# Four tail lanes, a shorter rounding to the 6-bit grid, and a re-costed planner in a two-layer transformer kernel

## Chip, core and metric

The kernel runs on one core of a Trainium2 chip. The metric is the device time of one execution in microseconds (us), the median of several executions. The engines are called as in the profile: PE (TensorE matmuls, with PEld its weight loads), DVE (VectorE), ACT (ScalarE), POOL (GpSimd) and SP (SyncE, which issues most DMAs).

## What is computed

Input `x` has 8 batches of 512 tokens with 128 features. All of it is float32. Two layers are applied; each batch is independent except for the routing, whose results do not depend on how batches are grouped.

```python
# layer 0: for each of two uses of the same experts, with attention between them
z = layernorm(x)
x = x + 0.5 * moe(z)          # 8 experts, best 2 of 8 by router logits, softmax over the two
x = x + attention(layernorm(x))  # 16 heads of width 8, rotary positions, causal softmax
x = x + 0.5 * moe(layernorm(x))
# moe: h = relu(z @ W1[e] + b1[e]); y = h @ W2[e] + b2[e]; weighted by the gate
# layer 1, the "tail": mx linear, gated scan block with its own ffn, mx linear
x = x + 0.5 * mxlinear(layernorm(x))
x = x + gated(layernorm(x))
x = x + 0.5 * mxlinear(layernorm(x))
# mxlinear: blocks of 32 features, scale = max|block| / 7.5,
#   q = nearest value on the 64-value grid (3 mantissa bits, 2 exponent bits; ties to the lower value)
#   out = (q * scale) @ (weight, quantized the same way).T + bias
# gated: xn = rmsnorm(z); a = 0.998 * sigmoid(xn Wd + bd) + 0.001
#   h_t = a_t h_(t-1) + sigmoid(xn Wg + bg) * tanh(xn Wv + bv)      (scan over the 512 tokens)
#   z2 = z + h;  out = z2 + Wout(silu(rms(z2) Wgate) * (rms(z2) Wup))
```

## The kernel before

**Stages.** The work is cut into stages, each a chain of steps on given engines (table `STAGES`: a letter for the engine and a cost in us, with `+` for what lands later and `<` for other predecessors). The mixture of experts (MoE) runs in six phases (`ORDER`): use 1 of batches 0-1, 2-4, 5-7 and use 2 of batches 0-2, 3-5, 6-7. A phase routes its tokens (`prep`, `route`), writes them with indirect DMAs on POOL into slots sorted by expert in HBM (`scat`, L1481), works through blocks of 256 slots, of which there are 106 in all (`wload` loads the expert's weights, 1 MB, into one of four buffers `wt`; `zin` loads and transposes the tokens; `hid` is one half of the hidden layer, two to a block; `res` the second matmul; `yout` transposes back and stores), and gathers the results with indirect DMAs on POOL (`comb`, L1493). Attention has the stages `proj`, `stack`, `maxi`, `mrow`, `scor`, `val` and `heads`; the last instruction of a batch's attention is the addition at L1131. Weights are split once at the start into two halves of float32r and stored in HBM scratch (`sload`, `split`).

**Order.** `timetable()` simulates all steps with their costs, a greedy list scheduler with the longest remaining chain as priority. Its result is one list of steps; every engine's program is the part of the list with its letter, written out in that order (`follow`). The engines are in order, so an instruction that waits holds up all behind it on its engine. `follows()` gives the dependences between stages and `bank_of` assigns the six shared PSUM banks.

**Tail.** The tail of a batch is `mxa`, then `gated`, then `mxb` (L1183-1263 on DVE, L1395-1450 on ACT, L1519-1556 on POOL, L815-868 on PE). It works in six buffers `tb[b % 2]` of 128x512 and small statistics in `sm_f[b % 2]`. There are two such sets ("lanes"): batch b waits for `mxb` of batch b-2. In an mx unit (there are 16, two a batch) ACT normalizes, DVE finds the block maxima (`scaled`, L1134-1141), POOL multiplies by the reciprocals (L1531), ACT takes the absolute value (L1405), DVE rounds with nine operations on 128x512 (`nearest`, L1143-1162), POOL multiplies by the scales (L1535), and adds half the bias to x (L1538), PE transposes and multiplies with the quantized weight, DVE adds to x (L1205). In `gated`, after the scan, DVE takes the mean square of z2 with bn_stats (L902, called at L1238-1239), and three small operations (L1242-1246); the unit ends in the addition to x at L1262.

**Start.** SP issues, in this order, the small inputs, ten DMAs that fill the slot scratch with zeros (L468), the first four expert loads (L487-488), the loads of the later inputs (`later`), and then alternates stores of split weights (L495) with the other four expert loads. All stages that need zeros wait for one semaphore that counts all ten.

```python
for f in range(2):
    for i in range(0, SLOTS, 1024):
        n = min(1024, SLOTS - i)
        e.dma_start(zd[f][i:i + n]..., zeros[...]).then_inc(l_zero, 16)
```

## Time and profile before

| what | value |
|---|---|
| median of 3 executions | 1385.29 us (1380.07 to 1401.86) |
| the profiled execution | 1396.99 us |
| its span in the profile | 1395.3 us |
| PE busy | 1012.7 us, 73% |
| DVE busy | 873.2 us, 63% |
| ACT busy | 628.3 us, 45% |
| POOL busy | 537.5 us, 39% |
| granted PE clock, mean | 0.849 of full speed |
| HBM traffic | 217.33 MB, mean 156 GB/s |

The span is measured on the profiler's clock from first to last event; the execution's own time is 1.7 us longer. Busy times of engines overlap, so they don't add up to the span. A "releaser" is what ended an engine's wait.

### The profile page before, as it was taken

The numbers are of one execution on the slowest core, as the hardware profiler recorded it, in microseconds if no ns is written. First come the engines' busy times: TensorE is split into PE (matmuls) and PEld (weight loads), VectorE is DVE, ScalarE is ACT, GpSimd is POOL, SyncE is SP. The second block draws the span as 40 slices with busy tenths as digits, with TensorE's granted clock in tenths as the row PEclk, the third lists the DMA queues.
The fourth block names the chain that finished last, engine by engine and source line by source line (L and its number), as shares of the span: only waits on it lengthen the run. The fifth ranks groups of instructions, "written<-read, shape, count | busy, mean of one in ns | idle before, by whom it ended". The sixth has DMA issues, their size and how long they took to land.

```text
span 1395.3 us, 21086 instructions
## 1 busy us (share of the span) xinstructions
PE 1012.7 (73%) x6869; PEld 717.2 (51%) x6869; DVE 873.2 (63%) x2457; ACT 628.3 (45%) x1341; POOL 537.5 (39%) x730
## 2 busy tenths in 40 slices
PE   1058885879899997799899648989991386664273
PEld 1048875655655764346567635646571356643132
DVE  5536474647665767457564446866659777858646
ACT  2135653345464664345467324636751363452241
POOL 2424245227221125565122472332428722344312
PEclk9999997899898998589899869968995698886576
DMA  9958987664554533534355756714114243410000
GB/s 334 353 211 289 320 297 238 210 222 145 164 173 137 171 108 87 175 113 133 107 167 192 262 153 192 239 61 135 54 54 158 68 152 117 163 29 14 15 0 16
DMA packets 84461, 217.33 MB, mean 156 GB/s; under 512 B 14848, under 2 KB 43392, under 8 KB 69760
## 3 DMA queue, kind: packets, MB, share of 16 engines
q1 hardware_dynamic: 76160, 199.18, 42.6%
q0 software_dynamic: 8192, 16.79, 4.1%
q8 instruction: 56, 0.92, 0.3%
q14 instruction: 53, 0.43, 0.1%
HBM read 160.86 MB, written 54.53 MB: 154 GB/s over the span
## 4 chain that ended last, share of the span: by engine, by line
PE 52%; DVE 11%; DMA 11%; issue 9%; POOL 8%; ACT 5%; SPq 4%; POOLq 0%; DVEq 0%; ACTq 0%
PE bank L584 46%; PE bank L596 5%; POOL z_scratch L1481 4%; DMA Qs<-q_scratch 4%; DMA q_scratch<-ab 2%; DMA tb<-in_wr 1%; DMA zin<-z_scratch 1%; SPq L542 1%; POOL yg L1493 1%; DVE sm_m L1090 1%; SPq L554 1%; DMA z_scratch<-zb,pos 1%; ACT tb L1277 1%; DMA k_scratch<-ab 1%; PE bank L731 1%
## 5 line engine op out<-in xcount | busy, mean ns | idle before, releaser
L1090 DVE TENSOR_REDUCE sm_m<-bank 128x4 f32<-128x512 f32 x320 | 212.1, 684 | 114.2 <-PE bank L584 113.9
L1515 POOL TENSOR_SCALAR_AFFINE_SELECT P<-P 128x256 f32<-128x256 f32 (+1 forms) x320 | 118.7, 377 | 348.4 <-ACT P L1367 344.8
L1367 ACT ACTIVATE P<-bank 128x512 f32<-128x512 f32 x320 | 179.8, 598 | 104.2 <-PE bank L584 103.4
L584 PE MATMUL bank<-zh,wt 128*128 128x256 f32 x1272 | 203.5, 310 | 14.9 <-DVE zh L1021 5.8
L1029 DVE SCALAR_TENSOR_TENSOR hlo<-bank,hhi 128x512 fp32r<-128x512 f32 x212 | 144.4, 687 | 101.9 <-ACT hhi L1316 101.2
L584 PEld LDWEIGHTS bank<-zh,wt 128*128 128x128 f32 x1272 | 178.8, 210 | 27.5 <-issue 12.3
L1316 ACT ACTIVATE hhi<-bank 128x512 fp32r<-128x512 f32 x212 | 125.9, 598 | 102.8 <-PE bank L584 97.2
L584 PE MATMUL bank<-hhi,wt 128*128 128x256 f32 x848 | 160.1, 313 | 5.4 <-ACT yb L1324 5.4
L1481 POOL DMA_INDIRECT z_scratch<-zb,pos x128 | 128.8, 1006 | 84.3 <-DVE pos L1010 49.2
L1493 POOL DMA_INDIRECT yg<-y_scratch,pos x128 | 124.6, 974 | 90.6 <-issue 54.1
L584 PE MATMUL bank<-Ks,Qs 32*128 32x256 f32 (+2 forms) x512 | 110.3, 447 | 66.7 <-DMA Qs<-q_scratch 53.6
L584 PEld LDWEIGHTS bank<-hhi,wt 128*128 128x128 f32 x848 | 121.9, 200 | 20.1 <-issue 18.1
L596 PE MATMUL bank<-ident,tb 128*128 128x128 f32 x160 | 34.0, 352 | 135.0 <-POOL tb L1535 99.8
L584 PEld LDWEIGHTS bank<-Ks,Qs 32*128 32x128 f32 x512 | 50.1, 200 | 120.9 <-issue 46.6
L584 PE MATMUL bank<-Qs,Ks 34*128 34x256 f32 (+2 forms) x512 | 87.2, 411 | 24.6 <-DVE sm_m L1090 10.5
L584 PE MATMUL bank<-P,Va 128*16 128x512 f32 (+3 forms) x1024 | 99.7, 488 | 0.0
L596 PEld LDWEIGHTS bank<-ident,tb 128*128 128x128 f32 x160 | 23.7, 180 | 145.4 <-issue 61.1
L1324 ACT ACTIVATE yb<-bank,wt 128x256 f32<-128x256 f32 x106 | 50.3, 474 | 106.7 <-PE bank L584 106.2
L584 PE MATMUL bank<-hlo,wt 128*128 128x256 f32 x424 | 89.0, 292 | 11.6 <-DVE hlo L1029 11.6
L584 PEld LDWEIGHTS bank<-Qs,Ks 34*128 34x128 f32 x512 | 45.3, 203 | 64.1 <-issue 31.5
L584 PEld LDWEIGHTS bank<-hlo,wt 128*128 128x128 f32 x424 | 68.8, 199 | 13.0 <-DVE hlo L1029 13.0
L584 PE MATMUL bank<-mask,identb 128*128 128x128 bf16 x512 | 72.5, 238 | 0.0
(184 smaller groups left out, 1694.6 us busy)
## 6 DMA issues: line engine op xcount, KB each, us to landing
wt<-w_scratch SPq DMA_DIRECT2D x106, 1025.0 KB, 6.5
zin<-z_scratch SPq DMA_DIRECT2D x106, 128.0 KB
y_scratch<-yt SPq DMA_DIRECT2D x106, 128.0 KB
w_scratch<-wt SPq DMA_DIRECT2D x8, 1024.0 KB, 9.3
q_scratch<-ab SPq DMA_DIRECT2D x32, 256.0 KB
k_scratch<-ab SPq DMA_DIRECT2D x32, 256.0 KB
Ks<-k_scratch SPq DMA_DIRECT2D x64, 128.0 KB, 2.8
Qs<-q_scratch SPq DMA_DIRECT2D x64, 128.0 KB, 3.1
```

The source lines that it names most:

```text
L542: e.dma_start(dst[par, :, 8 * r:8 * r + 8, :], (ab[3], ab[0])[low][:, :]).then_inc(s_qk[par], 16)
L554: e.dma_start(dst[64 * s_:64 * s_ + 32, :, :].bitcast(F32), src[b % 2, HH * g + s_:HH * g + HH:2].rearrange("p r t -> r p t")).then_inc(l_ ...
L584: return e.matmul(o, lhs, rhs, start=start, stop=stop, **kw)
L596: t = e.transpose(o[:, j * 128:(j + 1) * 128], src[:, j, :], ident[:, :])
L1029: e.scalar_tensor_tensor(out=hlo[s % 4][:, :, :].rearrange("p c t -> p (c t)"), in0=shared("hid", s, 0), scalar=0.0, in1=hhi[s % 4][:, :, ...
L1090: e.tensor_reduce(bn_m[:, k, s_, :], blocks(shared("maxi", i, 0, s_)), AX.X, ALU.max).then_inc(*d_max.step(i, f"m{s_}"))
L1316: e.activation(hhi[s % 4][:, :, :].rearrange("p c t -> p (c t)"), shared("hid", s, 0), ACT.Relu).then_inc(*a_hid.step(s, "hi"))
L1324: e.activation(yb[u % 2][:, :], y_bank[:, 0:SB], ACT.Identity, bias=wt[u % WR][:, 2048:2049].bitcast(F32)).then_inc(*a_yout.step(u, "y"))
L1367: e.activation(P[:, (2 * i + s_) % PR, :], shared("scor", i, 0, s_), ACT.Exp, scale=SCALE).then_inc(*a_sc.step(i, f"e{s_}"))
L1481: e.indirect_dma_start(zd[f % 2], bass.IndirectOffsetOnAxis(ap=pos[:, f % 2, k, i:i + 1], axis=0), zb[:, q % ZR, i % 4, :], None).then_inc ...
L1493: e.indirect_dma_start(yg[t % YR][:, k, :], None, yd[f % 2][0:SB * PHASE[f].blocks], bass.IndirectOffsetOnAxis(ap=pos[:, f % 2, k, i:i + 1 ...
L1515: e.affine_select(out=v, in_=v, compare_op=ALU.is_ge, fill=0.0, base=0, channel_multiplier=-1, pattern=pattern).then_inc(*p_sc.step(i, f"m ...
```

## The change

The diff does seven things.

1. The tail gets four lanes instead of two. Lanes 0 and 1 have five buffers `tb` each, lanes 2 and 3 lie in `P`, the buffer of attention's exponentials, and their first step waits for the last `val`. `TAIL_LANE` names each batch's lane; a batch waits for the one before it in its lane.
2. `nearest` is written anew with seven operations: the bits of the exponent are masked out and bounded by 1.0 (two one-input operations), and five operations with two inputs do the rounding. It needs no absolute value, so the ACT step L1405 goes. It works in three buffers.
3. The bias of the mx linear is added by PE: one more 128x512 matmul of `top` (a matrix with ones in its first row) with the bias, into the bank of the product. The POOL step L1538 goes.
4. The mean square of z2 comes from four ACT activations (Square, with the sum as second output), in place of bn_stats, bn_aggr and two small operations on DVE.
5. The zero fill is split: four DMAs of phase 0's slots, after the first four expert loads; the other six after all eight, behind `later`. Each part has its own semaphore.
6. All costs in `STAGES` are new. SP's steps cost by bytes (a weight load was 0.3 and is 2.6, a store of q or k was 0.4 and is 3.2), most PE steps cost more (`hid` 0.72, now 0.94), many DVE steps less.
7. Small things: raw rows of the eight expert loads go through four places of which one is in `tb0`; the memsets of `Ks` move behind the first routing; six slot limits instead of four are compared in `route` (L998).

```diff
+def pieces_of(f, start, end):
+    return [(f, i, min(1024, end - i)) for i in range(start, end, 1024)]
+FIRST_FILL = pieces_of(0, 0, PHASE[0].blocks * SB)
+LATER_FILL = pieces_of(0, PHASE[0].blocks * SB, SLOTS) + pieces_of(1, 0, SLOTS)
+TAIL_LANE = (0, 1, 0, 2, 3, 1, 0, 2)
+TAILS = max(TAIL_LANE) + 1
+def lane_before(b):
+    return max([p for p in range(b) if TAIL_LANE[p] == TAIL_LANE[b]], default=-1)
...
-    "wload": ("S.3+6", [], 1),
-    "hid": ("P.72 A.6 D.7", [(0, 2)], 1),
+    "wload": ("S2.6+4", [], 1),
+    "hid": ("P0.94 A0.58 D0.66", [(0, 2)], 1),
...
+                lane = TAIL_LANE[u] if stage in ("mxa", "gated", "mxb") else u % lanes
...
-        tb = [[sb(f"tb{i}{j}", [128, 4, 128]) for j in range(6)] for i in range(2)]
+        tb = [[sb(f"tb{i}{j}", [128, 4, 128]) for j in range(5)] for i in range(2)]
+        lane_t = [[t[:, :, :] for t in lane] for lane in tb]
+        lane_t += [[P[:, 5 * i + j, :].rearrange("p (j c) -> p j c", c=128) for j in range(5)] for i in range(2)]
...
+                if n == SG - 1:
+                    fill(FIRST_FILL, l_zero0)
+                if n == NE - 1:
                     later()
+                    fill(LATER_FILL, l_zero)
...
+                    mm(blocks(o), top[:, :], biasb.unsqueeze(1).to_broadcast([128, 4, 128]), True, False, skip_group_check=True)
                     w.wait_ge(*a_wq.at(0, "w"))
                     w.wait_ge(*a_mx[v].at(b, "zt"))
...
-                e.tensor_scalar(p, r, 2.0, 0.125, ALU.is_ge, ALU.mult).then_inc(*f.step(u_, "p"))
-                e.tensor_scalar(q, r, 4.0, 0.25, ALU.is_ge, ALU.mult).then_inc(*f.step(u_, "q"))
-                e.scalar_tensor_tensor(out=st, in0=p, scalar=0.125, in1=q, op0=ALU.add, op1=ALU.add).then_inc(*f.step(u_, "st"))
-                e.scalar_tensor_tensor(out=p, in0=st, scalar=MAGIC, in1=u, op0=ALU.mult, op1=ALU.add).then_inc(*f.step(u_, "r1"))
-                e.scalar_tensor_tensor(out=r, in0=st, scalar=-MAGIC, in1=p, op0=ALU.mult, op1=ALU.add).then_inc(*f.step(u_, "r2"))
-                e.tensor_tensor(p, r, u, ALU.subtract).then_inc(*f.step(u_, "d1"))
-                e.scalar_tensor_tensor(out=q, in0=p, scalar=2.0, in1=st, op0=ALU.mult, op1=ALU.is_ge).then_inc(*f.step(u_, "d2"))
-                e.tensor_tensor(q, q, st, ALU.mult).then_inc(*f.step(u_, "d3"))
-                e.tensor_tensor(r, r, q, ALU.subtract).then_inc(*f.step(u_, "d4"))
+                e.tensor_scalar(r.bitcast(U32), u.bitcast(U32), 0x7F800000, None, ALU.bitwise_and).then_inc(*f.step(u_, "p"))
+                e.tensor_scalar(r, r, 1.0, None, ALU.max).then_inc(*f.step(u_, "e"))
+                e.scalar_tensor_tensor(out=t, in0=r, scalar=MAGIC / 8, in1=u, op0=ALU.mult, op1=ALU.add).then_inc(*f.step(u_, "r1"))
+                e.scalar_tensor_tensor(out=u, in0=r, scalar=(MAGIC + 1) / 8, in1=u, op0=ALU.mult, op1=ALU.add
+                                       ).then_inc(*f.step(u_, "r2"))
+                e.scalar_tensor_tensor(out=u, in0=r, scalar=-0.125, in1=u, op0=ALU.mult, op1=ALU.add).then_inc(*f.step(u_, "r3"))
+                e.scalar_tensor_tensor(out=t, in0=t, scalar=1.0, in1=u, op0=ALU.mult, op1=ALU.min).then_inc(*f.step(u_, "mn"))
+                e.scalar_tensor_tensor(out=t, in0=r, scalar=-MAGIC / 8, in1=t, op0=ALU.mult, op1=ALU.add).then_inc(*f.step(u_, "r"))
...
-                stats(T[0], sm_, f, b, ("bn3", "ag3"))
-                e.tensor_tensor(t_, mv[:, :, 0], mv[:, :, 0], ALU.mult).then_inc(*f.step(b, "t4"))
-                e.tensor_tensor(t_, t_, mv[:, :, 1], ALU.add).then_inc(*f.step(b, "t5"))
+                w.wait_ge(*a_ga.at(b, "sq"))
+                e.tensor_scalar(t_, t_, 1.0 / D, 1e-6, ALU.mult, ALU.add).then_inc(*f.step(b, "t6"))
...
+                for j in range(4):
+                    t = e.activation(T[4][:, j, :], T[0][:, j, :], ACT.Square, accum_out=sm_[:, 44 + j:45 + j])
...
-                e.activation(flat(T[5]), flat(T[1]), ACT.Abs).then_inc(*f.step(b, "abs"))
-                e.tensor_tensor(x, x, hbias.unsqueeze(1).to_broadcast([128, 4, 128]), ALU.add).then_inc(*f.step(b, "x"))
```

**What moves.** The first place is SP's start. `z_scratch` is the slot memory, `w_scratch` the split weights, `P<-in_w` and `tb<-in_wr` the raw weights of an expert. Before:

```order
L463 DMA tb<-in_wt 128x128
L468 DMA z_scratch<-P 128x1024 x4
L468 DMA z_scratch<-P 128x768
L468 DMA z_scratch<-P 128x1024 x4
L468 DMA z_scratch<-P 128x768
L470 DMA w_scratch<-small 128x8x2
L487 DMA P<-in_w 128x1024
```

And in the changed kernel, from the same place (of the four expert loads the last is shown):

```order
L505 DMA tb<-in_wt 128x128
L507 DMA w_scratch<-small 128x8x2
L529 DMA P<-in_w 128x1024
...
L530 DMA tb<-in_wr 128x512
L512 DMA z_scratch<-P 128x1024 x3
L512 DMA z_scratch<-P 128x768
L540 DMA w_scratch<-wt 128x2048 x3
```

The first expert load stands in front of the zeros instead of behind all ten of them, and only four fills stand before the first weight store.

The second place is PE where attention ends: `wo,ob` is its last product, of batch 7; `zin` and `yb` are transposes of a block, `zh`, `hhi` and `hlo` its products, `tb` a tail buffer. Before:

```order
L584 MATMUL bank0<-tb02,wga 128x512
L584 MATMUL bank6<-tb12,wga 128x512
L584 MATMUL bank2<-hhi2,wt1 128x256 x4
L584 MATMUL bank2<-hlo2,wt1 128x256 x2
L584 MATMUL bank1<-wo,ob 128x128 x4
L584 MATMUL bank3<-zh0,wt2 128x256 x6
L584 MATMUL bank2<-hhi3,wt1 128x256 x4
L584 MATMUL bank2<-hlo3,wt1 128x256 x2
```

In the changed kernel:

```order
L629 MATMUL bank2<-hhi3,wt1 128x256 x4
L629 MATMUL bank2<-hlo3,wt1 128x256 x2
L641 MATMUL bank6<-ident,yb0 128x128 x2
L629 MATMUL bank0<-wo,ob 128x128 x4
L641 MATMUL bank4<-ident,zin0 128x128 x2
L641 MATMUL bank7<-ident,zb 128x128 x4
L641 MATMUL bank1<-ident,yb1 128x128 x2
L641 MATMUL bank3<-ident,zin1 128x128 x2
```

Before, two batches were already in the middle of `gated` here (`tb02,wga`), and 30 of the 212 `hid` halves stood behind this place; now no `gated` has begun, and 46 halves stand behind it, of phases 4 and 5.

The third place is PE near the end. `tb0x` is lane 0, `tb1x` lane 1, `P` lanes 2 and 3; `wdT` is the mx weight, `wg3` and `wga` weights of `gated`. Before, the last `mxa` units and the start of the last two `gated`:

```order
L584 MATMUL bank3<-wdT,tb01 128x128 x4
L596 MATMUL bank4<-ident,tb10 128x128 x4
L584 MATMUL bank0<-wdT,tb11 128x128 x4
L596 MATMUL bank6<-ident,tb01 128x128 x4
L596 MATMUL bank1<-ident,tb11 128x128 x4
L584 MATMUL bank7<-tb02,wg3 128x512
L584 MATMUL bank3<-tb12,wg3 128x512
```

Now:

```order
L629 MATMUL bank7<-P,wga 128x512
L641 MATMUL bank0<-ident,tb01 128x128 x4
L629 MATMUL bank4<-P,wup 128x512
L641 MATMUL bank1<-ident,tb11 128x128 x4
L629 MATMUL bank0<-tb02,wg3 128x512
L641 MATMUL bank1<-ident,P 128x128 x4
L629 MATMUL bank0<-tb12,wg3 128x512
L629 MATMUL bank1<-P,wg3 128x512
```

Three batches (6, 5 and 7) begin `gated` together, while a fourth (batch 4, `P,wga`) is in its second half; before it was two at a time. Behind the last `zin` stand the tails of batches 4 to 7 whole, and the ends of 1, 2 and 3.

## Rows read from the trace of the kernel before

**Rows 1.** Busy time by stretch: start:end, length, PE, PEld, DVE, ACT, POOL, PEclk, DMA, GB/s.
```profile
870.00:1040.00 170.00, 158.17 (x1097) 101.92 (x1096) 112.88 (x296) 103.17 (x219) 53.61 (x96) 0.89 0.34 111
1040.00:1130.00 90.00, 36.96 (x231) 30.56 (x230) 74.28 (x220) 30.47 (x69) 62.61 (x60) 0.68 0.36 119
1130.00:1240.00 110.00, 80.56 (x491) 66.55 (x490) 82.57 (x203) 54.64 (x123) 29.17 (x26) 0.87 0.34 118
1240.00:1396.00 156.00, 70.53 (x260) 44.41 (x260) 100.54 (x257) 42.65 (x92) 55.62 (x51) 0.63 0.05 14
```

**Rows 2.** Waits after 1040 us: who for whom, total us, times, longest.
```profile
PE bank L596 <- POOL tb L1535: 99.8, 8, 24.1
```

**Rows 3.** Timeline of DVE: start, us, instruction; ends of attention and of lane pairs.
```profile
1030.14 0.69 DVE L1131 TENSOR_TENSOR xs<-xs,bank 128x512 f32<-128x512 f32 x1 [0.22 <-PE bank L584]
...
1293.42 0.69 DVE L1205 SCALAR_TENSOR_TENSOR xs<-bank,xs 128x512 f32<-128x512 f32 x1 [1.85 <-PE bank L584]
...
1391.14 0.69 DVE L1205 SCALAR_TENSOR_TENSOR xs<-bank,xs 128x512 f32<-128x512 f32 x1 [3.38 <-PE bank L584]
```

**Rows 4.** Timeline of the start: SP's queue and the first block on PE.
```profile
16.34 1.47 SPq L487 DMA_DIRECT2D P<-in_w  x1
...
73.50 4.47 SPq L529 DMA_DIRECT2D wt<-w_scratch  x4
...
87.70 0.69 PE L596 MATMUL bank<-ident,zin 128*128 128x128 f32 x2 [3.50 <-DMA zin<-z_scratch]
```

**Rows 5.** PE busy by tile: wt, then yb (whole span), tb (870:1040), tb (870:1396).
```profile
0.00:1396.00 1396.00, 404.90 (x2544) 0.85 0.47 156
...
0.00:1396.00 1396.00, 43.35 (x212) 0.85 0.47 156
...
870.00:1040.00 170.00, 27.24 (x93) 0.89 0.34 111
...
870.00:1396.00 526.00, 157.82 (x624) 0.77 0.26 85
```

**Rows 6.** PE groups, whole span: busy, mean ns; two records to a matmul.
```profile
L584 PE MATMUL bank<-tb,wg 128*128 128x512 f32 x48 | 24.2, 635 | 0.8 <-ACT tb L1426 0.8
```

**Rows 7.** DVE groups, 870:1396: busy us, mean ns, idle before.
```profile
L1160 DVE TENSOR_TENSOR tb<-tb 128x512 f32<-128x512 f32 x16 | 18.0, 1127 | 0.5
...
L1158 DVE SCALAR_TENSOR_TENSOR tb<-tb 128x512 f32<-128x512 f32 x16 | 14.7, 919 | 0.6
...
L1151 DVE SCALAR_TENSOR_TENSOR tb<-tb 128x512 f32<-128x512 f32 x16 | 12.2, 762 | 0.5
...
L1153 DVE SCALAR_TENSOR_TENSOR tb<-tb 128x512 f32<-128x512 f32 x16 | 11.1, 692 | 0.5
...
L902 DVE BATCH_NORM_STATS2 sm_f<-tb 128x6 f32<-128x128 f32 x32 | 7.0, 281 | 0.3
...
L1147 DVE TENSOR_SCALAR tb<-tb 128x512 f32<-128x512 f32 x16 | 6.7, 418 | 0.0
```

**Rows 8.** DVE busy by tile: hlo (whole span), then tb (870:1040).
```profile
0.00:1396.00 1396.00, 144.36 (x212) 0.85 0.47 156
...
870.00:1040.00 170.00, 29.14 (x48) 0.89 0.34 111
```

**Rows 9.** POOL groups, whole span: busy us, mean ns, idle before and releasers.
```profile
L1493 POOL DMA_INDIRECT yg<-y_scratch,pos x128 | 124.6, 974 | 90.6 <-issue 54.1 <-DMA y_scratch<-yt 31.0 <-DVE xs L1044 3.6
```

**Rows 10.** Timeline of POOL and DVE in the last mx units.
```profile
1283.95 1.43 POOL L1535 TENSOR_TENSOR tb<-tb,sm_f 128x512 f32<-128x512 f32 x1 [8.51 <-DVE tb L1162]
...
1285.96 1.64 DVE L1160 TENSOR_TENSOR tb<-tb 128x512 f32<-128x512 f32 x1
```

**Rows 11.** Waits before 1040 us: who for whom, total us, times, longest.
```profile
PE bank L584 <- DMA Qs<-q_scratch: 53.6, 11, 25.4
```

**Rows 12.** ACT on yb by stretch; the count is of MoE blocks finished.
```profile
1040.00:1130.00 90.00, 0.94 (x2) 0.68 0.36 119
1130.00:1240.00 110.00, 6.12 (x13) 0.87 0.34 118
```

More of the change, by code:

```diff
@@ L187, in timetable @@
             share, _, late = item[1:].partition("+")
-            steps.append((item[0], float(share), float(late or 0.15), [int(x) for x in after.split(",")] if after else [k - 1]))
+            steps.append((item[0], float(share), float(late or 0.12), [int(x) for x in after.split(",")] if after else [k - 1]))
         plan[stage] = (steps, {x[0]: len(x) - 1 for x in holds}, {b: (x[0], i) for x in holds for i, b in enumerate(x[1:])})
@@ L191, in timetable @@
             for k, step in enumerate(steps):
-                queues.setdefault((stage, u % lanes, step[0]), []).append((u, k))
+                lane = TAIL_LANE[u] if stage in ("mxa", "gated", "mxb") else u % lanes
+                queues.setdefault((stage, lane, step[0]), []).append((u, k))
     before, after = {}, {}
@@ L290, in sem, with flow, tail_flow @@
             return ctx.enter_context(nc.semaphore(name))
-        def flow(name, steps, lanes=1):
-            return Flow([sem(f"{name}_{i}") for i in range(lanes)], steps)
+        def flow(name, steps, lanes=1, lane_of=None):
+            return Flow([sem(f"{name}_{i}") for i in range(lanes)], steps, lane_of)
+        def tail_flow(name, steps):
+            return flow(name, steps, TAILS, TAIL_LANE)
         bank = [ctx.enter_context(nc.psum_tensor(f"bank{i}", [128, 512], F32)) for i in range(8)]
@@ L463, in begin, with fill @@
                 e.dma_start(flat(tb[0][1])[:, 0:128], a["wt"]).then_inc(l_const, 16)
-                w.wait_ge(*p_init.at(0, "zero"))
-                for f in range(2):
-                    for i in range(0, SLOTS, 1024):
-                        n = min(1024, SLOTS - i)
-                        e.dma_start(zd[f][i:i + n].rearrange("(p j) d -> p j d", p=128), zeros[:, 0:n // 128, :]).then_inc(l_zero, 16)
                 w.wait_ge(l_first, 64)
                 e.dma_start(wd[:, 2048:WROW].rearrange("(e p) c -> p e c", p=128), bt).then_inc(s_bias, 16)
+            def fill(parts, done):
+                w.wait_ge(*p_init.at(0, "zero"))
+                for f, i, n in parts:
+                    e.dma_start(zd[f][i:i + n].rearrange("(p j) d -> p j d", p=128), zeros[:, 0:n // 128, :]).then_inc(done, 16)
             def later():
@@ L1015, in route @@
                 e.tensor_scalar(ei[:, f % 2, :], fl, part, None, ALU.add).then_inc(*g.step(f, "ei"))
+                if f == 0:
+                    for i in range(QR):
+                        e.memset(Ks[i][32:34, :, :].bitcast(F32), 1.0)
+                        t = e.memset(Ks[i][96:98, :, :].bitcast(F32), 1.0)
+                    t.then_inc(*d_init.step(0, "keys"))
                 yield
@@ L1625 @@
     small[:, 44] = g["L1_attn_rms_ffn_w"]
[L1626 removed]
+    small[:, 45:45 + EB] = SB * np.arange(EB)[None, :]
     small[:, 0:KB] = np.arange(KB)[None, :]
```

227 lines of the change are left out of this document (116 added, 111 removed), and 41 rows, old and new, of the table STAGES.

## The prediction

> **What bounds the kernel now.** I read the table of stretches first, then the waits after 1040 us, then DVE's timeline for the ends of units. The reader is to see two kernels in one. Up to the end of attention, whose last addition is at 1030.1 us [rows 3], PE sets the pace: in the last stretch before, it is busy 158.2 of 170 us, a share of 0.93 [rows 1]. From 1040 on no engine is full. PE is busy 37.0, 80.6 and 70.5 of 90, 110 and 156 us, DVE 74.3, 82.6 and 100.5, and the granted clock falls to 0.68 and 0.63 where PE is least busy [rows 1]. PE waits there 99.8 us for the multiplication by the scales on POOL, which comes behind the rounding on DVE [rows 2]. That is a chain of dependent steps, and only two batches at a time are allowed to be in it. The last pair shows its length: from the end of the pair before (the L1205 at 1293.4) to its own end (1391.1) it is 97.7 us [rows 3], and the pairs follow one another. So 356 us go by with some 190 us of PE's work and 257 of DVE's.
>
> **The change part by part.**
>
> *Start.* The first expert load is issued at 16.3 us behind the zeros; the split weights are read back from 73.5 on, and the first block is transposed at 87.7 [rows 4]. The bytes to move before the first weights can be read are nearly the same as before, since all eight stores must be done. So at most the way from 73.5 plus a load's landing to 87.7 is open. I bound the gain by 0 and 14 us and take 5, by the third of it in which routing and scatter no longer come last. The moved `Ks` memsets and the wider compare in the routing count for nothing: they lie under the loads.
>
> *Attention's end.* The new order leaves 46 `hid` halves behind attention instead of 30, that is 8 blocks more, and moves the parts of batches 0 and 1 behind it. A block costs PE (404.9 + 2 x 43.4) / 106 = 4.64 us, where `zin` is taken to cost what `yb` does [rows 5]; 8 of them are 37.1. The tail's matmuls before 1040 are 27.2 [rows 5]. With PE at 0.93 this comes off about one to one: 1030.1 - 37.1 - 27.2 - 5 = 960.8. What the new costs do to the order inside the first 960 us I set at zero, with -54 us as one end (all of PE's waits for `Qs` gone [rows 11]) and +30 as the other, half of those waits added.
>
> *Work behind it.* PE has 23 blocks x 4.64 = 106.7, the tail's 157.8 [rows 5], and the sixteen new bias products. Such a product is a 128x512 matmul; of that form 24 cost 24.2 us busy [rows 6], so 16 cost 16.1. It stands before the wait for the transposed input and can be done early, but it is PE's time all the same. The sum is 280.6.
> DVE has today's 257.4 [rows 1], the 29.1 of batches 0 and 1 [rows 8], 8 blocks at 144.4 / 106 = 1.36 for the residue of the hidden layer [rows 8], and loses: the old rounding costs 2 x 0.42 + 4 x 0.70 + 0.76 + 0.92 + 1.13 = 6.45 a unit, where 0.70 stands for L1149, L1153, L1156 and L1162, of which L1153 is shown [rows 7]. The new one costs 2 x 0.42 + 5 x 0.69 = 4.30, if masking bits costs what L1147 does. The trace has no such integer operation: its bounds are 0.42 and 0.69 (an operation with two inputs), and I take 0.42 because it also has one input in SBUF; the other end adds 16 x 0.27 = 4.3 us of DVE. The gain is 16 x 2.15 = 34.4, and 7.0 for the statistics of z2 [rows 7]. DVE's sum is 257.4 + 29.1 + 10.9 - 41.4 = 256.0, so PE is now the fuller engine, though by little. ACT loses its absolute values and gets 32 small Squares; POOL loses 16 additions of x. Neither is near its limit (54.6 of 110 us for ACT at its fullest in the tail [rows 1]), so I put nothing for them. The Squares stand in the chain in place of the statistics: both have four operations on 128x128, and I call it even.
>
> *Four lanes.* A waiting step of a lane is now covered by three others. The new wait of lanes 2 and 3 for the last `val` costs nothing, since no batch of theirs is ready before attention ends. How full can PE be? The bounds are the two rows: 0.93 in the attention stretch and 80.6 / 110 = 0.73, the best that two lanes with blocks beside them reach [rows 1]. I take 0.85, nearer to the row in which PE has as many independent chains. 280.6 / 0.85 = 330.1.
>
> *Sum.* 960.8 + 330.1 = 1290.9; from the last addition to the end of the span it is 1395.3 - 1391.8 = 3.5 us now, and the execution's own time is 1.7 longer than the span: 1296.1. The profiled execution (1396.99) lies 0.8% above the median (1385.29), so against the median the forecast is 1285. With 0.93 it is 1257, with 0.73 it is 1339. Between those ends lies the forecast's own range, 1257 to 1339.
>
> *A cross-check by the chain.* Before the last block PE has the 106.7 and about two batches' tail, 2 x 174 / 8 = 43.5, which at 0.93 end at 960.8 + 161.5 = 1122. Sixteen gathers at 0.97 + 0.30 us [rows 9] bring 1143. Then batches 5, 6 and 7 run together: the pair's 97.7 less 4 x 2.15 for the rounding is 89, and a third batch adds half of its DVE work, some 13. That ends at 1245 and makes 1240 by the median: the chain no longer sets the end, but it is not far away, and one cannot come below it by filling PE better.
>
> **The ports of DVE and POOL.** In the last mx units a subtraction-like operation of DVE took 1.64 us beside POOL's L1535 at 1.43 [rows 10], against 0.69 for the undisturbed form [rows 7]; the means of L1158 and L1160, 0.92 and 1.13, hold such cases. The new rounding has five such operations in a row with two inputs, and four lanes put more of POOL's products beside them. The price by rows: 32 products, each of which stretches one operation by 1.64 - 0.69 = 0.95, are 30 us of DVE, and (256 + 30) / 0.85 = 336, 6 us over the forecast's 330; if half of it also falls on the chain, 21 us.
> The Trainium skill, page "SBUF — State Buffer", section "Who interferes with whom", says that a DVE instruction with two SBUF inputs contends with a GpSimd instruction that reads SBUF, and that the later one is blocked until the other is done. The trace agrees for this pair. By that rule every product of POOL hits the rounding of some other lane, and the time would be the 1306 of the rival below.
>
> **The rivals.**
> *A, the front gains too.* For it: PE waited 53.6 us in eleven places for `Qs` [rows 11], and the new costs give the DMAs of q and k real lengths. Against it: the data are needed when they are, and PE is at 0.93 in the last stretch already. It gives 1285 - 53 = 1232.
> *B, the ports.* As above: 1285 + 21 = 1306. For it are rows 10; against it is that a third of POOL's tail work (the additions of x) goes.
> *C, the lanes do not overlap.* PE and DVE are both near 0.85 by my sum, the engines are in order, and one late step of one lane holds up the three others. For it: two lanes reached only 0.73 with blocks beside them [rows 1]. Then the gain is that of the shorter units and of 0.73: 1339. This is also the time if the change doesn't do what it says.
> *D, slower.* 23 blocks now run behind attention, in the same queues as the tails. If each is held up by a tail's waiting step in front of it on PE, the last `comb` is late, and three batches' tails come behind it. In 1040 to 1130 just 2 blocks were finished in 90 us, in 1130 to 1240 it was 13 in 110, 8.5 us each [rows 12]. At 8.5 the last block is done at 960.8 + 195 = 1156, harmless. With T for the last block's end, the time is T + 21 + 102 + 5.2, so 1413 by the median (1425 by the profiled one) is reached at T = 1297, 14.6 us a block. At 15 it is 1422. Against it: a wait of a lane used to be long because there was no other, and this is what the change fills.
>
> **How the numbers follow.** Chances: the forecast 0.58, A 0.14, B 0.08, C 0.14, D 0.06. The predicted time is 1285. The range 1228 to 1348 takes in the forecast's 1257 to 1339, A and B, and C with its upper neighbours; it leaves out D, and the far side of A, with the start's full 14 us. A difference of 2% is about what a measurement of this kernel can tell from no change, so the borders are 1357.6 and 1413. Faster: 0.58 + 0.14 + 0.08 and most of C, 0.91. The same: what is left of C and the mild side of D, 0.04. Slower: 0.05.
>
> **What would show it.** The last addition of attention should come near 961 us (935 to 990). If it stays near 1030, the step on the 8 blocks is wrong; if it is near 910, A is right. Behind it PE should be busy about 280 us at a share of 0.85, with a granted clock over 0.8; a share under 0.75 means C. The wait of PE for POOL's product by the scales should fall from 99.8 to under 40 us. The rounding's two-input operations should have means near 0.69; 0.9 and more means B. `zin` should be reached first near 83 us. DVE's sum over the span should fall from 873 to about 830. The last `comb` should be over before 1170; after 1290, D is right. The prediction is wrong if the time is above 1348 although attention ended before 990, since then the fill of the tail was misjudged.

## The result and the profile after

Before, the median is 1389.09 us over 4 executions (1380.07 to 1401.86); the changed kernel's is 1266.72 over 4 (1255.51 to 1273.9). The ratio is 0.913, with a 95% interval of 0.903 to 0.924: faster by 8.7%. The forecast was 1285, a ratio of 0.928.

The profiled execution took 1273.9 us, its span is 1272.2. These are lines of its page, the last one PE's busy tenths in 40 slices:

```profile
span 1272.2 us, 21017 instructions
PE 1025.4 (81%) x6901; PEld 716.8 (56%) x6901; DVE 829.4 (65%) x2344; ACT 622.9 (49%) x1388; POOL 507.7 (40%) x714
PE   1048789688999999879999996988999789853884
```

The longest waits of PE up to the end of attention, and the one for `Qs` (who for whom, total us, times, longest):

```profile
PE bank L641 <- ACT zb L1319: 51.3, 5, 35.6
PE bank L641 <- DMA zin<-z_scratch: 31.2, 8, 13.8
...
PE bank L629 <- DMA Qs<-q_scratch: 4.8, 1, 4.8
```

PE has 13 us more work than before (1025.4 against 1012.7) in 123 us less time. The wait for `Qs` that was 53.6 us [rows 11] is 4.8. The next rows are the table of stretches, with the columns of [rows 1]: up to attention's last addition, from there to the last gather, the rest, and the last two together.

```profile
0.00:955.00 955.00, 791.49 (x5569) 541.14 (x5569) 580.26 (x1680) 457.71 (x967) 373.09 (x585) 0.88 0.57 192
955.00:1119.00 164.00, 142.79 (x902) 115.06 (x903) 124.92 (x353) 103.14 (x261) 84.16 (x85) 0.96 0.58 197
1119.00:1272.00 153.00, 91.08 (x431) 60.59 (x429) 124.22 (x313) 62.01 (x163) 50.46 (x46) 0.81 0.04 13
955.00:1272.00 317.00, 233.88 (x1332) 175.64 (x1332) 249.15 (x665) 165.15 (x423) 134.62 (x130) 0.89 0.32 108
```

The same cut of the kernel before:

```profile
0.00:1031.00 1031.00, 815.63 (x5846) 569.64 (x5847) 609.09 (x1761) 495.21 (x1047) 389.04 (x593) 0.89 0.56 186
1031.00:1396.00 365.00, 197.06 (x1025) 147.54 (x1023) 264.08 (x697) 133.13 (x295) 148.41 (x137) 0.72 0.21 71
```

Of the 123 us by which the span is shorter, 76 were won before attention's end and 47 behind it. In front, PE's busy time fell by only 24 us (815.6 to 791.5), but its idle time fell by 52 (215.4 to 163.5). Behind, PE does 37 us more work in 47 us less, and the granted clock is 0.89 instead of 0.72. As in [rows 1], the clock fell where PE is least busy: 0.96 with PE at 0.87, 0.81 with PE at 0.60.

The part with blocks beside the tails (955 to 1119) is nearly full now. The last 153 us are not. This is their table of stretches:

```profile
1119.00:1130.00 11.00, 9.63 (x79) 8.78 (x77) 10.18 (x41) 5.37 (x14) 3.95 (x4) 1.00 0.02 6
1130.00:1182.00 52.00, 19.60 (x84) 13.13 (x84) 49.67 (x116) 14.64 (x40) 19.69 (x18) 0.70 0.04 16
1182.00:1243.00 61.00, 51.18 (x218) 30.76 (x218) 42.32 (x116) 35.66 (x97) 18.68 (x18) 0.92 0.00 1
1243.00:1272.00 29.00, 10.67 (x51) 7.92 (x50) 22.05 (x44) 6.35 (x15) 8.15 (x7) 0.69 0.10 36
```

Batches go through the tail in threes, in step. From 1130 to 1182 six mx units come in two groups of three (the last of three batches, the first of three others): DVE is busy 49.7 of 52 us and PE 19.6. Then the last three batches and one more are in `gated`, and PE is busy 51.2 of 61 us. In the last three mx units it is DVE again, 22.1 of 29, and PE 10.7. The step shows on DVE's timeline:

```profile
1250.99 1.15 DVE L1198 TENSOR_SCALAR tb<-tb 128x512 f32<-128x512 f32 x1
1252.17 0.69 DVE L1200 SCALAR_TENSOR_TENSOR tb<-tb 128x512 f32<-128x512 f32 x1
1252.78 0.42 DVE L1196 TENSOR_SCALAR P<-P 128x512 uint32<-128x512 uint32 x1
1253.23 0.43 DVE L1198 TENSOR_SCALAR P<-P 128x512 f32<-128x512 f32 x1
...
1257.09 0.68 DVE L1202 SCALAR_TENSOR_TENSOR tb<-tb 128x512 f32<-128x512 f32 x1
1257.80 1.42 DVE L1205 SCALAR_TENSOR_TENSOR tb<-tb 128x512 f32<-128x512 f32 x1
...
1268.27 0.69 DVE L1250 SCALAR_TENSOR_TENSOR xs<-bank,xs 128x512 f32<-128x512 f32 x1 [1.59 <-PE bank L629]
```

The roundings of three batches stand directly behind one another, and DVE hardly waits; the last line is the kernel's last addition. PE's timeline shows the other side, one wait for each group of three:

```profile
1144.84 1.09 PE L641 MATMUL bank<-ident,tb 128*128 128x128 f32 x4 [11.85 <-POOL tb L1577]
...
1173.64 1.09 PE L641 MATMUL bank<-ident,tb 128*128 128x128 f32 x4 [17.65 <-POOL tb L1577]
...
1258.73 1.11 PE L641 MATMUL bank<-ident,tb 128*128 128x128 f32 x4 [14.57 <-POOL tb L1577]
```

### The profile page after: what moved, and what is told of

It is laid out like the page before. It is cut to its first block, busy times and chain, and to the rows that moved or that the text cites. A ratio compares the mean times of both kernels' runs of the same rounds, so it can differ in the third digit from the quotient of the medians.

```text
span 1272.2 us, 21017 instructions
## 1 busy us (share of the span) xinstructions
PE 1025.4 (81%) x6901; PEld 716.8 (56%) x6901; DVE 829.4 (65%) x2344; ACT 622.9 (49%) x1388; POOL 507.7 (40%) x714
## 4 chain that ended last, share of the span: by engine, by line
PE 42%; DVE 20%; DMA 13%; issue 8%; ACT 7%; POOL 6%; SPq 5%; DVEq 0%; ACTq 0%; POOLq 0%
PE bank L629 37%; PE bank L641 4%; DMA yg<-y_scratch,pos 3%; DMA zin<-z_scratch 2%; POOL z_scratch L1525 2%; DMA q_scratch<-ab 2%; DVE hlo L1079 2%; DVE sm_m L1140 2%; POOL yg L1537 2%; DMA w_scratch<-wt 2%; SPq L587 1%; PE bank L776 1%; SPq L610 1%; ACT P L1410 1%; ACT zb L1319 1%
## 5 line engine op out<-in xcount | busy, mean ns | idle before, releaser
L1140 DVE TENSOR_REDUCE sm_m<-bank 128x4 f32<-128x512 f32 x320 | 209.3, 684 | 101.6 <-PE bank L629 100.9
L1410 ACT ACTIVATE P<-bank 128x512 f32<-128x512 f32 x320 | 174.8, 594 | 110.6 <-PE bank L629 110.2
L629 PE MATMUL bank<-zh,wt 128*128 128x256 f32 x1272 | 209.1, 314 | 19.4 <-DVE zh L1071 13.3
L1559 POOL TENSOR_SCALAR_AFFINE_SELECT P<-P 128x256 f32<-128x256 f32 (+1 forms) x320 | 115.6, 369 | 228.9 <-ACT P L1410 223.9
L629 PEld LDWEIGHTS bank<-zh,wt 128*128 128x128 f32 x1272 | 182.5, 213 | 43.2 <-DVE zh L1071 18.2
L1525 POOL DMA_INDIRECT z_scratch<-zb,pos x128 | 126.0, 985 | 128.0 <-DVE pos L1055 93.1
L629 PE MATMUL bank<-Ks,Qs 32*128 32x256 f32 (+2 forms) x512 | 114.9, 466 | 9.8 <-DMA Qs<-q_scratch 4.8
L629 PE MATMUL bank<-Qs,Ks 34*128 34x256 f32 (+2 forms) x512 | 92.1, 424 | 20.5 <-DVE ab L1121 8.8
L1071 DVE TENSOR_TENSOR zh<-bank,zh 128x256 fp32r<-128x256 f32 x106 | 43.0, 419 | 63.9 <-ACT zh L1351 63.9
L1372 ACT ACTIVATE yt<-bank 128x256 f32<-128x256 f32 x106 | 40.4, 381 | 77.8 <-PE bank L641 69.7
## 6 DMA issues: line engine op xcount, KB each, us to landing
q_scratch<-ab SPq DMA_DIRECT2D x32, 256.0 KB, 3.9
k_scratch<-ab SPq DMA_DIRECT2D x32, 256.0 KB, 3.5
```

The lines of the kernel that those rows point to most:

```text
L629: return e.matmul(o, lhs, rhs, start=start, stop=stop, **kw)
L1071: e.tensor_tensor(z[:, 1, :], shared("zin", u, 1)[:, 0:SB], z[:, 0, :].bitcast(F32), ALU.subtract).then_inc(*d_zin.step(u, "lo"))
L1140: e.tensor_reduce(bn_m[:, k, s_, :], blocks(shared("maxi", i, 0, s_)), AX.X, ALU.max).then_inc(*d_max.step(i, f"m{s_}"))
L1372: e.activation(flat(yt[u % 2]), shared("yout", u, 1)[:, 0:SB], ACT.Copy).then_inc(*a_yout.step(u, "t"))
L1410: e.activation(P[:, (2 * i + s_) % PR, :], shared("scor", i, 0, s_), ACT.Exp, scale=SCALE).then_inc(*a_sc.step(i, f"e{s_}"))
L1525: e.indirect_dma_start(zd[f % 2], bass.IndirectOffsetOnAxis(ap=pos[:, f % 2, k, i:i + 1], axis=0), zb[:, q % ZR, i % 4, :], None).then_inc ...
```

## The experiments

Each ratio is to the kernel before on the same chip. Runs 1 to 4 were on one chip, where the kernel before takes 1395 us, runs 5 to 8 on a second (1454 us) and runs 9 to 12 on a third (1456 us). The changed kernel itself was run again only on the second, where its ratio is 0.918 (0.910 to 0.926) instead of 0.913: the ratios stand together though the times don't. Runs 9 to 12 are compared with it by ratios alone. One per cent of the ratio is about 14 us. Every edit of a cost or a step also changes the planned order, unless the run says that it keeps it.

**1. Two lanes.** All the change except the lanes.

```diff
-TAIL_LANE = (0, 1, 0, 2, 3, 1, 0, 2)
+TAIL_LANE = (0, 1, 0, 1, 0, 1, 0, 1)
```

> The changed kernel with two tail lanes instead of four (TAIL_LANE = 0,1,0,1,...), all else kept, the planner included. Theory 1 (the lanes are the larger part of the tail's gain): the last four pairs follow one another again, each some 8 to 10 us shorter than the 98 us of before; the time is 1325 to 1350. Rival (the shorter units and the new costs did it, the lanes little): 1270 to 1295.

Measured: 1313.41 us, ratio 0.944 (0.936 to 0.951). That lies between the two forecasts: the lanes count, but for less than theory 1 had them.

**2. Old costs.** The changed kernel with the old numbers in `STAGES` for all stages but `wquant` and the tail's (`mxa`, `gated`, `mxb`), which keep the new ones.

```diff
-    "wload": ("S2.6+4", [], 1),
-    "hid": ("P0.94 A0.58 D0.66", [(0, 2)], 1),
+    "wload": ("S.3+6", [], 1),
+    "hid": ("P.72 A.6 D.7", [(0, 2)], 1),
```

> The changed kernel with the old costs for all stages but the tail's and wquant, which change the order alone. Theory 1 (the new costs bring the front nothing that matters): 1260 to 1290, and PE's waits for Qs may come back without the time. Rival (rival A of the prediction: the front gains by them): 1300 to 1340, with the 54 us of waits for Qs back in the trace and the end of attention after 980 us.

Measured: 1316.96 us, ratio 0.943 (0.935 to 0.951). PE waits 29.3 us for `Qs`, ten times. The time is the rival's; of its signs, 29 of the 54 us of waits came back, and attention ends at 974, not after 980.

**3. New costs alone.** The kernel before with the new numbers and nothing else.

```diff
-    "wload": ("S.3+6", [], 1),
-    "hid": ("P.72 A.6 D.7", [(0, 2)], 1),
+    "wload": ("S2.6+4", [], 1),
+    "hid": ("P0.94 A0.58 D0.66", [(0, 2)], 1),
```

> The kernel before with only the new costs (in its tail the same kind of costs on its own steps); two lanes, old rounding. Theory 1: the order alone is worth under 30 us, so 1360 to 1395; the rival has 1320 to 1355. Together with old_costs it says whether the gain of the costs depends on the lanes.

Measured: 1357.51 us, ratio 0.973 (0.966 to 0.979). The wait for `Qs` is 1.4 us. The time falls between the two forecasts: the order that the costs give is worth 38 us where theory 1 had under 30. This is its table of stretches, cut at attention's end:

```profile
0.00:976.00 976.00, 808.04 (x5747) 556.76 (x5748) 599.36 (x1721) 480.86 (x1020) 380.91 (x589) 0.90 0.58 194
976.00:1350.00 374.00, 216.99 (x1124) 161.29 (x1123) 277.98 (x737) 143.13 (x322) 154.55 (x141) 0.76 0.22 74
```

The first three runs together, from such tables:

| kernel | attention ends | PE idle before | behind it | ratio |
|---|---|---|---|---|
| before | 1031 | 215 | 365 | 1 |
| new costs alone | 976 | 168 | 374 | 0.973 |
| changed, two lanes | 951 | 157 | 348 | 0.944 |
| changed, old costs | 974 | 191 | 349 | 0.943 |
| changed | 955 | 164 | 317 | 0.913 |

Read down, the ratios split the gain: the new costs give 0.027 (38 us), the shorter units with the rest of the edits 0.029 (40 us, from 0.973 to 0.944), the four lanes 0.030 (42 us). Each difference is uncertain by 0.010 to 0.013, and each of these steps has a planned order of its own; a change of order alone cost up to 0.014 in runs 7 and 9 below. So the split says what each step brings together with its order. The table's spans are of single executions, 1298.9 us with two lanes and 1272.2 changed, so they differ by 27 us where the medians differ by 47. The costs alone bring attention's end forward by 55 us, of which PE's busy time explains 8 (815.6 to 808.0) and its idle time 47; but behind attention, with two lanes, nothing is won: 374 us instead of 365. The lanes work only behind attention: 348 to 317. Taking the costs out of the changed kernel (run 2) loses 0.030, about what they give alone, and most of that lies behind attention too: 349 instead of 317.

**4. Bias on POOL.** The changed kernel with the bias added by POOL as before, and no bias product. The planned costs go with it: PE's step of the mx unit is 0.9 instead of 1.8, and POOL has a step of 1.3 more.

```diff
-                    mm(blocks(o), top[:, :], biasb.unsqueeze(1).to_broadcast([128, 4, 128]), True, False, skip_group_check=True)
+                    e.tensor_tensor(x, x, hbias.unsqueeze(1).to_broadcast([128, 4, 128]), ALU.add).then_inc(*f.step(b, "x"))
```

> The changed kernel with half the bias added to x on POOL again, and without the sixteen bias products on PE. Theory 1 (DVE, at 249 of 317 us, and not PE, at 234, is the fuller engine behind attention, so 16 to 19 us less of PE buy nothing, while POOL's 20 us stretch DVE's two-input operations): 1265 to 1285. Rival (PE's work sets the tail, as the prediction's sum has it): 1245 to 1258.

Measured: 1292.53 us, ratio 0.929 (0.921 to 0.937), slower than both forecasts. The step costs 0.016 when undone, but which part of it?

**5. The changed kernel again**, without an edit, as the scale of the runs that follow.

> The changed kernel itself, as the mark for the three kernels beside it on the same chip: 0.905 to 0.92 of before.

Measured: 1336.57 us, ratio 0.918 (0.910 to 0.926).

**6. Bias in both places.** The planner's step on POOL with the addition, and the product on PE as well; the bias is counted twice in the result.

```diff
+                    e.tensor_tensor(x, x, hbias.unsqueeze(1).to_broadcast([128, 4, 128]), ALU.add).then_inc(*f.step(b, "x"))
```

> bias_pool (half the bias added on POOL, old share of the order) with the sixteen bias products put back on PE, in bias_pool's order; the bias is counted twice in the output. Theory K (the bias products, issued while PE would idle, keep its granted clock up, and that is what bias_pool lost): 10 to 20 us faster than bias_pool's 1292, with the clock of the last 150 us up from 0.73 to above 0.8. Theory P (POOL's addition, by its ports or its place in POOL's queue, is what bias_pool lost): as bias_pool or up to 5 us slower.

Measured: 1362.52 us, ratio 0.937 (0.928 to 0.947). Theory K's gain of 10 to 20 us over run 4 (0.929) didn't come.

**7. Bias in neither.** The planner's step on POOL is kept, with a memset of four columns in it; the bias is left out of the result. The edit is shown against run 4.

```diff
-                    e.tensor_tensor(x, x, hbias.unsqueeze(1).to_broadcast([128, 4, 128]), ALU.add).then_inc(*f.step(b, "x"))
+                    e.memset(sm_[:, 56:60], 0.0).then_inc(*f.step(b, "x"))
```

> bias_pool with POOL's addition shrunk to a memset of four elements: neither PE nor POOL adds the bias, which is left out of the output; the order is bias_pool's. Theory K: no faster than bias_pool by more than 5 us, since PE idles as there. Theory P: 10 to 20 us faster than bias_pool, near 1275.

Measured: 1354.35 us, ratio 0.930 (0.922 to 0.939). It does the least work of the three and is no faster than run 4, so theory P's gain of 10 to 20 us didn't come either. All three share one planned order, which has sixteen more POOL steps in it and a shorter cost for PE's step. These are the rows of stretches behind attention, of bias in neither and then of bias in both places, on the same chip:

```profile
1006.00:1354.00 348.00, 236.03 (x1313) 178.99 (x1311) 248.77 (x669) 166.76 (x424) 136.50 (x145) 0.83 0.30 99
```

```profile
1004.00:1358.00 354.00, 242.29 (x1341) 180.18 (x1338) 258.61 (x669) 166.61 (x424) 155.17 (x145) 0.86 0.29 97
```

Sixteen additions on POOL make DVE's busy time 9.8 us longer with the same 669 instructions, 0.6 us for each, and run 6 ends 8 us later than run 7, which the intervals don't separate. But even run 7 is 18 us slower than run 5, with no execution of the one inside the range of the other, so the work moved is not what counted. Theory K was right on the clock in part: behind attention it is 0.86 with the products and 0.83 without them, in the last 150 us 0.78 and 0.73. It bought no time. Run 9 takes the plan out of the question.

**8. Rounding shorter by two.** The operations r3 and mn are left out, in the same plan; ties are no longer rounded to the lower value.

```diff
-                e.scalar_tensor_tensor(out=u, in0=r, scalar=-0.125, in1=u, op0=ALU.mult, op1=ALU.add).then_inc(*f.step(u_, "r3"))
-                e.scalar_tensor_tensor(out=t, in0=t, scalar=1.0, in1=u, op0=ALU.mult, op1=ALU.min).then_inc(*f.step(u_, "mn"))
```

> The changed kernel with two of the rounding's five two-input operations left out (r3 and mn, so ties are rounded otherwise), 17 units less 2 x 0.69 = 22 us of DVE of which the order knows nothing. If DVE's work sets the tail (249 of 317 us busy): 15 to 25 us under after_again. If the chain of the last three lanes does: that chain holds the rounding of each of the three lanes twice, so 3 x 2 x 1.4 = 8 us. If PE does: under 4 us.

Measured: 1327.25 us, ratio 0.915 (0.905 to 0.924), so 9 us by the medians and 5 by the ratios, within the intervals. That doesn't tell the three cases of the expectation apart.

**9. The same order without the bias product.**

```diff
-                    mm(blocks(o), top[:, :], biasb.unsqueeze(1).to_broadcast([128, 4, 128]), True, False, skip_group_check=True)
```

> The changed kernel with every instruction in its place, but without PE's sixteen bias products; so the mx linear's bias is left out of the result. Theory K (the products lie in PE's idle time and cost nothing; what the runs without them lost came from the planner's other order): ratio within 5 us of the changed kernel, 0.909 to 0.922. Rival P (PE's work sets the tail): 12 to 16 us faster, a ratio of 0.902 to 0.908.

Measured: 1336.45 us, ratio 0.916 (0.911 to 0.921), and 0.918 with the product in run 5. The rival's 0.902 to 0.908 is outside the interval; the comparison, by ratios from two chips, is itself uncertain by 0.01, some 14 us. This is its row of stretches behind attention:

```profile
1002.00:1338.00 336.00, 235.49 (x1302) 180.34 (x1302) 249.94 (x665) 165.24 (x422) 134.52 (x130) 0.83 0.31 102
```

PE is busy 235.5 us, and 239.6 with the products (the row of run 5 stands in run 10), though their own records take 19 us there. The granted clock is 0.83 instead of 0.86. So theory K of this expectation stands in what it says of the time, within that: the products cost nothing that shows. Whether they lay in idle time, or whether leaving them out was paid back by the lower clock, this run doesn't tell. What run 7 lost against this run (0.930 to 0.916), with neither the product nor the addition in it, lies in its other order, with the sixteen small POOL steps and DVE's wait for them; these weren't taken apart.

**10. Rounding short, planned anew.** The operations r2, r3 and mn are left out, and the planner's cost of the step falls from 2.9 to 0.8. In the expectation "the kernel with one operation less" is run 8, which left out two.

```diff
-    "mxa": ("D1.4 G1.1 D0.2 A1.6 D1.1 G1.1 D2.2 D2.9 G1.4 P0.92 A0.6 P1.8 D0.7", [(9, 10), (11, 12)], TAILS),
+    "mxa": ("D1.4 G1.1 D0.2 A1.6 D1.1 G1.1 D2.2 D0.8 G1.4 P0.92 A0.6 P1.8 D0.7", [(9, 10), (11, 12)], TAILS),
...
-                e.scalar_tensor_tensor(out=u, in0=r, scalar=(MAGIC + 1) / 8, in1=u, op0=ALU.mult, op1=ALU.add
-                                       ).then_inc(*f.step(u_, "r2"))
...
```

> The changed kernel with the rounding cut to four operations: r2, r3 and mn go, so ties are rounded by the adder's own rule and not to the lower value; the planner's cost of the step falls from 2.9 to 0.8. DVE loses 16 x 2.1 = 34 us in the tail. Theory (chain and DVE set the tail together; the kernel with one operation less was 9 us faster for 22 us of DVE): 15 to 25 us faster than the changed kernel, ratio 0.898 to 0.907. Rival (PE at 0.74 of the tail is what sets it): under 5 us. Second rival (the other plan costs what the shorter chain gives, as with the bias): no faster or slower.

Measured: 1331.67 us, ratio 0.915 (0.911 to 0.920). A miss: some 4 us instead of 15 to 25, as both rivals had it. Its row of stretches behind attention, and the changed kernel's on the second chip (run 5):

```profile
999.00:1327.00 328.00, 241.01 (x1332) 180.84 (x1332) 224.30 (x623) 164.74 (x423) 135.76 (x130) 0.86 0.32 104
```

```profile
1001.00:1337.00 336.00, 239.63 (x1332) 178.86 (x1332) 249.48 (x665) 164.64 (x422) 134.62 (x130) 0.86 0.31 102
```

DVE loses 25 us there and the stretch becomes 8 us shorter. The expectation took DVE as the bound of the whole tail; by the table of the last 153 us it is that only in the mx stretches. The plan is another one too, so neither rival is excluded.

**11. Zeros first.** All ten fills stand ahead of the expert loads again; the planned order is unchanged.

```diff
                 if n == SG - 1:
-                    fill(FIRST_FILL, l_zero0)
-                if n == NE - 1:
                     later()
-                    fill(LATER_FILL, l_zero)
...
+            fill(FIRST_FILL, l_zero0)
+            fill(LATER_FILL, l_zero)
```

> The changed kernel with all ten zero fills ahead of the expert loads, as before; all else, the planned order too, is unchanged. Forecast from the prediction: the start's part of the gain was 5 us (3.8 measured at the first block). Theory S (the bytes before the first block are the same, only their order differs): the first block on PE comes 0 to 6 us later and the whole 0 to 6 us. Rival: routing and the first scatter come some 20 us later again (32 to 52 us), and the first block with them, 8 us and more.

Measured: 1340.44 us, ratio 0.919 (0.914 to 0.924). The first block is transposed at 85.2 us, and at 85.1 in run 5. Routing is 8 us later (the positions are written at 40.2 instead of 32.2), and the first block is no later for it. Theory S holds: the split of the zeros gave nothing that shows.

**12. Sums on DVE.** The mean square of z2 comes from bn_stats, bn_aggr and two small operations on DVE, as before; the Squares on ACT go.

```diff
-                    t = e.activation(T[4][:, j, :], T[0][:, j, :], ACT.Square, accum_out=sm_[:, 44 + j:45 + j])
+                stats(T[0], sm_, f, b, ("bn3", "ag3"))
+                e.tensor_tensor(t_, mv[:, :, 0], mv[:, :, 0], ALU.mult).then_inc(*f.step(b, "t4"))
+                e.tensor_tensor(t_, t_, mv[:, :, 1], ALU.add).then_inc(*f.step(b, "t5"))
```

> The changed kernel with the mean square of z2 on DVE again (bn_stats, bn_aggr and two small operations), without the 32 Squares on ACT, each of which was followed by a read of the accumulator of 187 ns that the prediction had not counted. DVE gets about 13 us more in the tail, ACT loses 15. Theory E (even, as predicted): within 5 us of the changed kernel. Rival (DVE at 0.79 behind attention sets the tail): 6 to 13 us slower, ratio 0.918 to 0.928.

Measured: 1351.21 us, ratio 0.927 (0.922 to 0.931), 0.008 above run 11 on the same chip, 11 us, as the rival said; the two intervals just touch. Against run 9 on that chip it is 0.011, clear of both intervals. Behind attention DVE is busy 263.3 of 346 us, 13.8 more than in run 5. But this run is planned anew as well, and runs 4, 6 and 7 show that a plan alone can cost as much, so it is not shown that the 13.8 us are the reason.

No run beats the changed kernel by more than its interval.

## Why the prediction came out as it did

The time is inside the range (1285 forecast, 1266.7 measured, range 1228 to 1348), and it was won where the forecast had it: attention ends earlier, and four lanes fill PE better behind it. But in each of the two parts two terms were wrong and cancelled, so that the parts came out this near is luck. Point by point:

*Attention's end, 960.8 forecast, 954.7 measured.* Right to 6 us, but for another reason. The step was: 37.1 us of blocks and 27.2 of the tail leave this part "about one to one", and "What the new costs do to the order inside the first 960 us I set at zero". The moves took place (82 blocks are finished before attention's end instead of 89, and 2.2 us of the tail's matmuls are left of 21.2), yet PE's busy time fell by 24 us and not by 64, and 52 us of idle time went. Part of the 64 was misread: the 27.2 ran to 1040, 9 us past attention's end, and only 21.2 of it lay in front. Added up by tile as the forecast did, the blocks and the tail left 28.6 and 19.0 us, 47.6; other matmuls of PE took longer in the new order (the products of `ab` with `wqk`, for one, had a mean of 660 ns instead of 625). Why they did is open. Run 3 shows the zero to be wrong: with the costs alone and two lanes, the idle time falls by 47. Rival A was right about its mechanism (PE's waits for `Qs` went from 53.6 to 4.8 us), and the forecast had credited nearly its size to work moved. The two errors cancel, by luck.

*Start, 5 us.* 3.8 measured (87.7 to 83.9). Run 11 shows that it doesn't come from the zeros; run 3, which still has them all in front, reaches its first block at 84.3. The changed kernel with the old costs (run 2) reaches it at 86.6. So most of it comes with the order that the new costs give.

*PE's work behind, 280.6 forecast, 233.9 measured.* This is the term that failed most. PE by tile, 955 to 1272, for `wt`, `tb`, `P`, `yb`, `zin` and `top` in this order:

```profile
955.00:1272.00 317.00, 86.24 (x576) 0.89 0.32 108
955.00:1272.00 317.00, 89.35 (x378) 0.89 0.32 108
955.00:1272.00 317.00, 51.35 (x234) 0.89 0.32 108
955.00:1272.00 317.00, 9.32 (x48) 0.89 0.32 108
955.00:1272.00 317.00, 7.33 (x44) 0.89 0.32 108
955.00:1272.00 317.00, 18.23 (x30) 0.89 0.32 108
```

They add up to 261.8, of which the blocks are 102.9 (forecast 106.7), the tail 140.7 (forecast 157.8, from rows in which the clock was 0.77), and the bias products 18.2 (16.1). PE's busy time in the same stretch is 233.9. So 19 us of the error lie in the groups themselves, mostly the tail's, read at a lower clock (0.77) than was granted now (0.89), which is the likely reason, and 28 are overlap: records of different groups lie over one another, and their busy times must not be added.

*Share 0.85.* 0.74 measured. The work was too high and the share too high: with the share alone put right the part would have been forecast at 380 us, with the work alone at 275. Together they gave 330.1 where 317 was measured, which is luck as well. The text had said that a share under 0.75 means rival C. It doesn't: that threshold rested on the 280.6. The row of 0.93 was a good guide only while blocks remain (142.8 of 164 us, 0.87); behind the last gather PE is at 0.60, since three batches are in the same stage at once and PE and DVE take turns.

*DVE's sum behind, 256.0.* 249.2 measured, and 829.4 over the span where "about 830" was forecast. But "so PE is now the fuller engine" is wrong: behind attention DVE is busy 249.2 of 317 us and PE 233.9, because PE's sum had been put too high. The masking took 0.39 and 0.42 us, as the end with one input had it.

*The cross-check by the chain.* The last gather was forecast 182 us behind attention's end (1143 less 960.8) and is 163 behind it. The way from there was forecast at 102 us and is 153, and this half failed: "a third batch adds half of its DVE work, some 13". It left out that the group of three has to wait for the group of three in front of it (whose mx units keep DVE busy from 1130 to 1157), and that its own units stand behind one another on DVE.

*Bias and sums.* The bias product was counted as 16.1 us of PE's work; run 9 takes all sixteen out, and PE is busy 4 us less and the time no shorter. The Squares were called even with the statistics; run 12 doesn't contradict it clearly, see there.

*Rival B.* Its price was read from the wrong pair. The timeline of before, where the 1.64 us stand:

```profile
1283.95 1.43 POOL L1535 TENSOR_TENSOR tb<-tb,sm_f 128x512 f32<-128x512 f32 x1 [8.51 <-DVE tb L1162]
1284.51 1.42 DVE L1158 SCALAR_TENSOR_TENSOR tb<-tb 128x512 f32<-128x512 f32 x1
1285.35 1.71 POOL L1538 TENSOR_TENSOR xs<-xs,small 128x512 f32<-128x512 f32 x1
1285.96 1.64 DVE L1160 TENSOR_TENSOR tb<-tb 128x512 f32<-128x512 f32 x1
```

L1535 had ended at 1285.38 when L1160 began. The 1.64 stand beside L1538, the addition of x that the change takes out; what L1535 stretches is L1158, to 1.42. The contention that the prediction cites is in the trace for both pairs, but a product by the scales costs DVE 1.42 - 0.69 = 0.73 us and not 0.95, and 1.42 is what L1205 takes now beside L1577. The rows of the rounding, whole span:

```profile
L1198 DVE TENSOR_SCALAR tb<-tb 128x512 f32<-128x512 f32 x10 | 8.6, 859 | 0.3
L1198 DVE TENSOR_SCALAR P<-P 128x512 f32<-128x512 f32 x6 | 2.6, 427 | 0.2
L1202 DVE SCALAR_TENSOR_TENSOR tb<-tb 128x512 f32<-128x512 f32 x10 | 6.8, 684 | 0.0
L1205 DVE SCALAR_TENSOR_TENSOR tb<-tb 128x512 f32<-128x512 f32 x10 | 9.2, 922 | 0.3
L1205 DVE SCALAR_TENSOR_TENSOR P<-P 128x512 f32<-128x512 f32 x6 | 6.3, 1056 | 0.2
```

Two of the seven operations are stretched and five are not: the excess is 10 x 0.43 for L1198, 10 x 0.23 and 6 x 0.36 for L1205, together 8.8 us of DVE and not 30. That every product of POOL hits the rounding of some other lane was too much. By the prediction's sign, a mean of 0.9 or more, L1205 alone speaks for B; the other four two-input operations have means of 0.68 to 0.70. L1198 has one input only and wasn't in the prediction's list; it took 1.15 us beside POOL's L1573 and 0.43 without it. The trace of before has the same case, in an operation that the prediction put at 0.42:

```profile
1274.40 1.05 POOL L1531 TENSOR_TENSOR tb<-tb,sm_f 128x512 f32<-128x512 f32 x1 [0.49 <-DVE sm_f L1141]
1274.60 1.13 DVE L1146 TENSOR_SCALAR tb<-tb 128x512 f32<-128x512 f32 x1 [0.28 <-ACT tb L1405]
```

The Trainium skill, page "SBUF — State Buffer", section "Who interferes with whom", counts DVE's two-port fast mode among what contends with GpSimd, beside two inputs; the trace agrees with that for L1198, whose 0.43 is well under the 0.69 of a two-input operation. POOL's side is stretched too: L1577 took 1.43 us beside L1205 and 1.05 elsewhere.

*Rivals C and D.* C fell by the time and by run 1: the lanes, with their order, are worth some 42 us. What C said of lanes that wait for one another is still seen in the last 153 us. D fell: the last gather is at 1118.

*The wait for POOL's product.* Forecast under 40, measured 44.1 for lanes 0 and 1 and 3.0 for lanes 2 and 3, which lie in `P`, instead of 99.8. The rows are the waits of the changed kernel after 955:

```profile
ACT tb L1447 <- PE bank L641: 45.4, 8, 12.3
PE bank L641 <- POOL tb L1577: 44.1, 3, 17.6
PE bank L641 <- POOL P L1577: 3.0, 2, 2.6
POOL tb L1577 <- DVE tb L1209: 32.4, 8, 5.4
```

The three waits of 44.1 us are those shown on PE's timeline above: the stretches in which DVE rounds for three batches.

What stays open: why the plan with sixteen more POOL steps loses 0.012 to 0.02, why PE's other matmuls took longer in front, and how much of the last 153 us a plan could save that keeps the three batches in different stages. The last wasn't tried.

## What to carry to other kernels

Never add busy times of groups to get an engine's work: take one row of the engine over the stretch, and scale it. Split what is won before a milestone into an engine's busy and idle time; a date can come out right with the reasons wrong. More lanes fill an engine while they are in different stages: here the last batches arrived together and ran in step, and two engines took turns. And when an experiment on a planned kernel changes the plan, compare it with one that keeps the old order, as the plan alone can be worth more than the edit.
